# ScalarE's exponentials of the newest attention unit ahead of its evictions of older units, in a gated cross-attention and FFN kernel

## What is computed

```
x = x + tanh(g_xattn) * attention(layernorm(x), context)
x = x + tanh(g_ffn)   * ffn(layernorm(x))
```

## Time and profile before

| | |
|---|---|
| runs | 2189.68, 2186.43, 2190.2 us |
| profiled execution, its own time | 2189.43 us |
| its span, first to last instruction | 2187.6 us |
| mean granted clock of TensorE | 0.995 |
| PE busy | 2116.5 us, 97% |
| DVE busy | 1307.6 us, 60% |
| ACT busy | 834.3 us, 38% |
| POOL busy | 198.8 us, 9% |
| DMA | 213.22 MB, mean 97 GB/s |

### The profile page before, as it was taken

The page is one execution under the profiler, slowest core; times in us unless marked ns, Lnnn a source line. Parts: engine busy times, 40 slices in busy tenths (PEclk is TensorE's granted clock), DMA queues, the critical chain, the costliest instruction groups (busy, mean ns, idle before and its releaser), DMA issues.

```text
span 2187.6 us, 29797 instructions
## 1 busy us (share of the span) xinstructions
PE 2116.5 (97%) x10208; PEld 1773.1 (81%) x10208; DVE 1307.6 (60%) x2175; ACT 834.3 (38%) x1956; POOL 198.8 (9%) x215
## 2 busy tenths in 40 slices
PE   7899999999999999999999999999999898999999
PEld 6788888888788888888878888888888787888887
DVE  6885544456687654445668765444558865445444
ACT  4772422222386332222248633322225753222321
POOL 1330000000033000000013200000002320000000
PEclk9999999999999999999999999999999999999999
DMA  5113522223212352222221243322223122223321
GB/s 183 59 45 130 183 86 86 87 96 106 103 53 78 111 178 96 87 88 88 92 108 53 85 147 131 115 86 86 87 77 126 39 87 96 87 86 115 115 77 58
DMA packets 58910, 213.22 MB, mean 97 GB/s; under 512 B 6449, under 2 KB 6449, under 8 KB 58801
## 3 DMA queue, kind: packets, MB, share of 16 engines
q1 hardware_dynamic: 58800, 211.84, 28.5%
HBM read 203.42 MB, written 8.39 MB: 97 GB/s over the span
## 4 chain that ended last, share of the span: by engine, by line
PE 80%; DVE 11%; issue 4%; ACT 4%; DMA 1%; SPq 0%; POOL 0%; DVEq 0%; ACTq 0%; POOLq 0%
PE ps L956 26%; PE ps L957 26%; PE ps L958 26%; DVE kb_h L681 2%; ACT pb L459 2%; DVE nmx L696 1%; DVE kb_l L683 1%; PE ps L996 1%; DVE pt_l L629 1%; DVE xt_l L629 1%; DVE qo_l L629 1%; DVE qo_l L667 1%; DVE qo_h L667 1%; PE ps L987 1%; DMA x<-in_x 1%
## 5 line engine op out<-in xcount | busy, mean ns | idle before, releaser
L956 PE MATMUL ps<-xt_h,wc_h 128*128 128x512 f32 x1184 | 466.6, 394 | 0.0
L957 PE MATMUL ps<-xt_l,wc_h 128*128 128x512 f32 x1184 | 462.9, 391 | 0.0
L958 PE MATMUL ps<-xt_h,wc_l 128*128 128x512 f32 x1184 | 462.3, 390 | 0.0
L629 DVE TENSOR_TENSOR wr_l<-wr_raw,wr_h 128x1024 fp32r<-128x1024 f32 (+1 forms) x112 | 139.5, 1245 | 368.4 <-ACT wr_h L403 368.3
L753 DVE SCALAR_TENSOR_TENSOR x<-ps,tg,x 128x512 f32<-128x512 f32 x352 | 257.5, 748 | 151.9 <-PE ps L958 151.9
L956 PE MATMUL ps<-wr_h,h_h 128*128 128x512 f32 x672 | 261.8, 390 | 0.4 <-DVE h_l L629 0.4
L957 PE MATMUL ps<-wr_l,h_h 128*128 128x512 f32 x672 | 261.5, 389 | 0.0
L958 PE MATMUL ps<-wr_h,h_l 128*128 128x512 f32 x672 | 261.5, 389 | 0.0
L958 PEld LDWEIGHTS ps<-xt_h,wc_l 128*128 128x128 f32 x1184 | 223.2, 189 | 47.1
L956 PEld LDWEIGHTS ps<-xt_h,wc_h 128*128 128x128 f32 x1184 | 223.6, 189 | 43.7
L957 PEld LDWEIGHTS ps<-xt_l,wc_h 128*128 128x128 f32 x1184 | 223.7, 189 | 43.5
(11 more groups left out here) (106 smaller groups left out, 3293.5 us busy)
## 6 DMA issues: line engine op xcount, KB each, us to landing
wc_raw<-in_wc SPq DMA_DIRECT2D x216, 512.0 KB, 4.2
wr_raw<-in_wr SPq DMA_DIRECT2D x112, 512.0 KB, 3.3
x<-in_x SPq DMA_DIRECT2D x5, 2048.0 KB, 8.7
out<-x SPq DMA_DIRECT2D x16, 512.0 KB, 3.1
ct_raw<-in_ctx_t SPq DMA_DIRECT2D x15, 512.0 KB, 5.2
xn<-in_x SPq DMA_DIRECT2D x3, 2048.0 KB, 10.2
wo_raw<-in_wr SPq DMA_DIRECT2D x8, 512.0 KB, 5.0
kv_raw<-in_wc SPq DMA_DIRECT2D x8, 256.0 KB, 5.4
```

The costliest lines, as they stand in the source:

```text
L629: return nc.vector.tensor_tensor(out, whole, hi.bitcast(F32), ALU.subtract)
L956: pe.matmul(out, w_h, m_h, start=first, stop=False)
L957: pe.matmul(out, w_h, m_l, start=False, stop=False)
L958: return pe.matmul(out, w_l, m_h, start=False, stop=last)
```

## The change

On ACT, in each step, the call of `exps(g, n)` moves from behind `o_out` and `pt_out` to ahead of them. The order on the other engines, and every wait, stay as they are.

```diff
--- before.py
+++ after.py
@@ -493,12 +493,12 @@
 
                 act.wait_ge(stored, g * (16 * NB) + 1)
                 for n in range(STEPS + 1):
+                    if n < UNITS:
+                        exps(g, n)
                     if n >= 7 and n % 2 == 1:
                         o_out(g, (n - 7) // 2)
                     if 3 <= n < UNITS + 3:
                         pt_out(g, n - 3)
-                    if n < UNITS:
-                        exps(g, n)
                     if n % 4 == 2 and n < UNITS - 8:
                         q_out(g, n // 4 + 2)
```

## The result

The changed kernel takes 2306.15 us (median of four runs, 2304.99 to 2307.89) against 2189.94 us before: 1.0533 times as long, 95% interval 1.0515 to 1.0552. The forecast was 2300 us, slower with 0.95.

A forecast was written before the change was run, and what follows sets the result against it. PE, 97% busy, bounded the kernel; afterwards a closed ACT-DVE loop would bound the attention. Stage 98.8 + tail 5.2 + clock 6.8 = 111 us on the profiled 2189.43 gave about 2300 us, range 2280 to 2326.

The forecast's parts named there:

- The loop: In each attention step, row maximum, exponentials, high part and low part run in strict turn: 3.36 us, 3.74 with output pair.
- The key blocks: Four attention steps (12, 13, 17, 20) also build a key block on DVE, each 2.40 us longer.
- What hides: Reciprocal, split or q eviction fit in DVE's and ACT's idle time at no cost; uncovered, 0.1 to 0.3 us each.
- PE's tie: From an output pair's low part through weigh to the row maximum two steps on: 6.65 us, 0.45 to spare.
- The sum: Attention steps 3 to 30 take 108.3 us a group, before 82.8 or 84.4: 98.8 us more in all.
- The tail without a fall: After the last row maximum (31), weigh 13 starts 3.09 us later instead of 1.78: 1.3 us a group, 5.2 in all.
- The clock: PE falls to half clock in each group's attention tail: 1.7 us a group, 6.8 in all, at least nothing.
- the clock becomes a bound: Rival, chance 0.08: clock falls at weigh steps 8, 10, 16 cost 3.7 us a group, 15 in all, 2315 us.
- The working of the tail's fall: PE idles about 4.2 us before weigh 13, its transpose of unit 29 ending about 6 us after row maximum 29.
- signs of being wrong: Wrong if successive row maxima stand under 3.3 us apart, DVE never waits for pt_h, or half clock exceeds a few steps.
- Half absorbed: Rival, chance 0.07: DVE's other odd-step work covers the later eviction, only 16 steps lengthen, 45 us in all, 2235 us.
- Faster: Rival, chance 0.03: earlier exponentials free other work and PE's 21 us of attention waits vanish, 2168 us.

## Why the forecast was right, point by point

**The loop** was right, and shown. Its links came from the old trace: from places where one engine happened to be waiting for the other, and from the pace of an engine that went from one instruction to the next without a wait. The new trace has 3.35 to 3.36 us against the 3.36, and 3.74 against the 3.74. Cutting it on DVE takes most of the loss away with the new order on ScalarE in place, and the same cut without the new order wins nothing.

**The key blocks** came out at 5.76 (12, 20) and 6.15 us (13, 17), against 3.36 or 3.74 + 2.40 = 5.76 and 6.14.

**What hides** did hide: splits and q evictions sit in the idle halves, and no step has an overhang from them.

**PE's tie** through the output pair has 0.45 us to spare in the forecast, and holds: at full clock no step is longer for it. With the loop cut it becomes the bound, at 6.66 us for steps 8 and 9.

**The sum** for the stage was 98.8 us more in four groups. With repeated transposes, where no fall lengthens a step, it is 4 x 108.2 - 334.4 = 98.4. The tail without a fall was 5.2 and is 4 x (12.44 - 11.12) = 5.3.

**The clock** is the mis-sized term: 6.8 us forecast, about 16 measured by stretches (440.1 - 432.8 = 7.3 in the stages, 8.7 in the tails), 14.3 by the run that fills the idle time. I had one fall of 3.4 us in each tail. In fact the tail of groups 0 and 1 ran 6.8 us at half clock, that of 2 and 3 one of 3.4, and falls came in the stage as well. From weigh 13 to weigh 15 the long fall cost 2.8 us and the short one 1.55, where the forecast had 1.7. The first row below is the stretch ahead of the fall in step 8 of group 1 of the changed kernel, the second the fall in its tail:

```profile
650.90:654.60 3.70, 1.63 (x11) 1.12 (x9) 2.75 (x5) 3.40 (x15) 1.73 (x2) 1.00 0.42 142
...
750.20:757.00 6.80, 6.12 (x23) 5.46 (x24) 5.71 (x12) 3.93 (x7) 1.04 (x1) 0.50 0.01 2
```

In the first PE was busy for 1.63 of 3.70 us, and the 3.4 us that followed were at half clock. Most falls in the stage cost nothing, as the loop is longer than PE's work; the one in step 8 of groups 0 to 3 added 0.8, 0.8, 2.4 and 1.1 us, the one in step 22 of groups 2 and 3 added 1.1 and 1.0. That is the mechanism of the rival "the clock becomes a bound": it had 15 us for the stage on top of the forecast, and came at about half of that, in step 8, which it had named, and in step 22, which it had not; steps 10 and 16, its other two, kept their length.

The working of the tail's fall was wrong too, though a fall did come. The forecast had PE idle for 4.2 us ahead of weigh 13, with the transposes of unit 29 done 6 us after row maximum 29 (740.69 in group 1). The trace:

```profile
748.01 0.63 PE L996 MATMUL ps<-ident,pb 128*128 128x128 f32 x4 [0.29 <-DVE pt_l L629]
750.88 0.55 PE L956 MATMUL ps<-pt_h,vp_h 128*128 128x256 f32 x1 [2.25 <-DVE qo_l L629]
```

Weigh 13 starts 10.2 us after row maximum 29, as forecast. But the transposes of unit 29 start only 7.3 us after it, since their bank is freed by a low part of DVE, which the forecast left out. The wait was 2.25 us, and the clock fell all the same.

One of the signs of being wrong that the prediction names was met: in each group PE was at half clock for 20.4 us of the stage, which is more than "a few of these steps". Yet apart from steps 8 and 22 the loop, and not the clock, set the length of the steps.

That 2306.15 lies only 6 us from the forecast is in part luck. In the profiled executions the time grew by 118.5 us, the medians by 116.2, against a forecast of 111: the profiled execution of the changed kernel is the slowest of its four.

The Trainium skill ("TensorE: Matmul & The Clock Gate", HAM oscillation) has a kernel whose bursts between waits start cold each time; its waits are for DMAs and longer than most of PE's waits here, of which the longest at each fall took 1.5 to 3.3 us. The trace agrees in part: 6 or 7 falls in a group of 16 pairs, not one in each.

**The rivals.** "Half absorbed" fell: odd steps lengthened as computed. "Faster" fell: PE's waits for qo_l rose from 5.3 to 18.2 us a group. PE did not wait for the exponentials at all. What I wrote of DVE's waits, over 30 us a group for pt_h, was too much, since on steps with a pair DVE waits for qo_h in its place; the two together are 38.2.

## What to carry to other kernels

When two engines pass work back and forth, each in a fixed order, draw the loop before moving an instruction: here "the newest first" on ScalarE put an eviction behind a wait for VectorE, whose own list had the next result behind that eviction, and a pipeline over 32 units turned into strict alternation. The price can be read from the old trace, link by link, above all from the few places where the follower was waiting already. A move on one engine has to be matched in the other's list, and even then it won nothing here. A likely reason, not tested by itself, is that ScalarE already waited for the row maximum in 12 of the 28 steps: there was little for earlier exponentials to win.

## What the runs showed of the hardware

TensorE's clock was the surprise: at each fall in the attention PE had just waited, or was waiting, for 1.5 to 3.3 us, and the granted clock was at half for 3.4 or 6.8 us at a time; 14 us came back by giving it useless transposes, although they add some 19 us of work a group. Four transposes of 128 x 128 in float32 take 0.46 us (24 in 2.78), twice what I had counted.
